# Inner order of three split-precision products in a kernel of graph blocks on one core

## What is computed

```python
def reference(x, adj, nodemask, ...):
    x = _layernorm(x + _L0_gnn_ref(x, adj, W))
    # relu([x, (adj @ x) / deg] @ W.T): x's own part plus the aggregate
    x = _layernorm(x + _L1_gnn_ref(x, adj, W1, b1, W2, b2, W3, b3))
    # three GCN layers: support = x @ W; adj @ support + b; relu after the first two
    x = _layernorm(x + _L2_gnn_ref(x, nodemask, adj, adj, W_qkv, W_out, b_out))
    # 8 heads of 64: softmax plus adjacency and exp(-distance) terms, times values
    x = _layernorm(x + _L3_gnn_ref(x, adj, W_qk, W_v))
    # one gate per node, softmax over the nodes, times values
```

## Time and profile before

| | |
|---|---|
| runs | 1280.2 us median, 1279.27 to 1281.15 |
| the profiled execution | 1280.6 us, span of the core 1278.7 us |
| mean granted TensorE clock | 0.998 of 2.4 GHz |
| TensorE matmuls | 98% of the span, 10732 matmuls and as many weight loads |
| VectorE, ScalarE, GpSimd | 90%, 75%, 14% |

### The profile page before, as it was taken

The page is one execution under the profiler, slowest core; times in us unless marked ns, Lnnn a source line. Parts: engine busy times, 40 slices in busy tenths (PEclk is TensorE's granted clock), DMA queues, the critical chain, the costliest instruction groups (busy, mean ns, idle before and its releaser), DMA issues.

```text
span 1278.7 us, 30231 instructions
## 1 busy us (share of the span) xinstructions
PE 1259.2 (98%) x10732; PEld 1156.0 (90%) x10732; DVE 1155.8 (90%) x3671; ACT 958.4 (75%) x2534; POOL 177.2 (14%) x383
## 2 busy tenths in 40 slices
PE   8999999999999999999999999999999999999997
PEld 7888999999999999999999999999999999999886
DVE  6988999999999999999999999999999999998895
ACT  6677678778778787777787787787787787787773
POOL 0001111101111101111111111011111011111011
PEclk9999999999999999999999999999999999999999
DMA  6110111110111100111100111101111101110000
GB/s 230 35 35 2 35 43 44 44 31 14 44 43 44 43 27 19 43 44 43 44 12 34 43 44 44 43 2 43 44 43 44 43 2 44 43 44 10 10 9 25
DMA packets 42659, 49.06 MB, mean 38 GB/s; under 512 B 16272, under 2 KB 25232, under 8 KB 42512
## 3 DMA queue, kind: packets, MB, share of 16 engines
q1 hardware_dynamic: 42512, 47.14, 11.7%
HBM read 38.68 MB, written 8.39 MB: 37 GB/s over the span
## 4 chain that ended last, share of the span: by engine, by line
PE 94%; DVE 2%; ACT 2%; DMA 1%; issue 1%; POOL 0%; SPq 0%; POOLq 0%; DVEq 0%
PE psum L1551 63%; PE psum L1565 11%; PE psum L1803 9%; PE psum L1761 8%; PE psum L1854 1%; PE psum L1857 1%; ACT work L578 1%; DMA adjT_sb<-in_adjT 0%; DVE bn L929 0%; DMA v_sb<-in_w 0%; DVE x L963 0%; DVE x_pre L1021 0%; POOL rstd L382 0%; DVE x_pre L1187 0%; DVE work L1092 0%
## 5 line engine op out<-in xcount | busy, mean ns | idle before, releaser
L578 ACT ACTIVATE work<-work,shift 128x256 f32<-128x256 f32 x512 | 253.7, 500 | 4.9 <-DVE shift L1092 4.8
L1111 DVE SCALAR_TENSOR_TENSOR work<-work,rsum,extra 128x256 f32<-128x256 f32 x512 | 216.8, 475 | 1.0
L1092 DVE CUSTOM_DVE_ANT_0 work<-psum,minus_big 128x256 f32<-128x256 f32 x512 | 189.0, 417 | 3.0 <-PE psum L1761 2.8
L429 ACT ACTIVATE work<-psum 128x512 f32<-128x512 f32 x256 | 138.0, 598 | 71.6 <-PE psum L1565 71.5
L379 POOL TENSOR_TENSOR mv<-mv,eps 128x2 f32<-128x2 f32 x128 | 31.0, 242 | 1081.7 <-DVE mv L950 1081.7
L1551 PE MATMUL psum<-x2T_h,wqkv_h 128*128 128x256 f32 x512 | 145.6, 284 | 0.0
L429 ACT ACTIVATE sup_h<-psum 128x512 fp32r<-128x512 f32 x124 | 73.2, 590 | 95.2 <-PE psum L1551 95.1
L1551 PE MATMUL psum<-x2T_h,wqkv_l 128*128 128x256 f32 x512 | 143.0, 279 | 0.0
L1551 PE MATMUL psum<-x2T_l,wqkv_h 128*128 128x256 f32 x512 | 142.9, 279 | 0.0
L1565 PE MATMUL psum<-ident,work 128*128 128x128 f32 x1024 | 127.4, 273 | 0.0
L1803 PE MATMUL psum<-work,v_sb 128*64 128x256 f32 x1024 | 124.6, 385 | 0.0
(11 more groups left out here) (189 smaller groups left out, 3798.5 us busy)
## 6 DMA issues: line engine op xcount, KB each, us to landing
xT_sb<-in_xT SPq DMA_DIRECT2D x32, 256.0 KB, 2.6
adjT_sb<-in_adjT SPq DMA_DIRECT2D x32, 256.0 KB, 3.0
adj_sb<-in_adj SPq DMA_DIRECT2D x32, 256.0 KB, 4.0
x_sb<-in_x SPq DMA_DIRECT2D x32, 256.0 KB, 4.3
out<-y_sb SPq DMA_DIRECT2D x32, 256.0 KB, 3.5
work<-in_wqkv SPq DMA_DIRECT2D x1, 1536.0 KB, 9.6
mask_row<-in_nodemask SPq DMA_DIRECT2D x32, 32.0 KB, 4.2
w_raw<-in_w SPq DMA_DIRECT2D x3, 256.0 KB, 5.4
```

The source lines that it names most:

```text
L429: return nc.scalar.activation(dst, src, ACT.Copy, scale=scale)
L578: last = nc.scalar.activation(prob[:, p % 2, i, h], prob[:, p % 2, i, h], ACT.Exp, bias=shift[:, p % 2, h, i:i + 1], scale=-1.0, accum_out ...
L1092: last = V_.tensor_tensor_reduce(out=prob[:, p % 2, i, h], in0=bank(SCORES[p] + h)[:, i * N:(i + 1) * N], in1=minus_big[:, g % 2, i], scal ...
L1111: last = V_.scalar_tensor_tensor(out=prob[:, p % 2, i, h], in0=prob[:, p % 2, i, h], scalar=rsum[:, p % 2, h, i:i + 1], in1=extra[:, g % 2 ...
```

## The change

A new function, `whole_product`, writes a product in one piece: for each t and k the matmuls Lh Rh, Lh Rl, Ll Rh in turn. `self_product` and `support` call it in place of the two parts. `support` loses its argument `part`, and all its waits, the one for the low half among them, stand ahead of its first matmul. All ten places that call `support` are changed alike: the two calls (HI, LO) become one in the same place. The first two of them are shown.

```diff
--- before.py
+++ after.py
@@ -1579,6 +1579,13 @@
                                    late[part], opens=part == HI and t == 0, closes=part == LO and t == NT - 1)
                 return last
 
+            def whole_product(dst, left, right):
+                for t in range(NT):
+                    last = product(dst[:, t * F:(t + 1) * F],
+                                   [(cut(left, A, k, block_of(t)), cut(right, A, k)) for k in range(FT)],
+                                   opens=t == 0, closes=t == NT - 1)
+                return last
+
             def weights(g, number):
                 if g == 0:
                     pe.wait_ge(dve_w, number)
@@ -1610,9 +1617,7 @@
                 weights(g, W0 + 1)
                 pe.wait_ge(dve_xT, once(g))
                 reuse(pe, act_self, once(g - 1))
-                for part in (HI, LO):
-                    last = nodes_product(bank(SELF), fT_of(g), [w[:, :, 0:F] for w in w0], part)
-                last.then_inc(pe_self, 1)
+                whole_product(bank(SELF), fT_of(g), [w[:, :, 0:F] for w in w0]).then_inc(pe_self, 1)
 
             def aggregate(g, part):
                 if not live(g):
@@ -1640,26 +1645,17 @@
                 if part == LO:
                     last.then_inc(pe_sup[0], 1)
 
-            def support(layer, g, part):
-                if not live(g):
-                    return
-                if part == HI:
-                    weights(g, W1 + layer)
-                    if layer == 2:
-                        reuse(pe, dve_qk, nth(g - 1, layer))
-                    if layer == 1:
-                        reuse(pe, dve_gate, once(g - 3))
-                        pe.wait_ge(act_hid_hi[0], once(g))
-                    if layer == 2:
-                        pe.wait_ge(act_hid_hi[1], once(g))
-                else:
-                    if layer == 1:
-                        pe.wait_ge(dve_hid[0], once(g))
-                    if layer == 2:
-                        pe.wait_ge(dve_hid[1], once(g))
-                last = nodes_product(bank(SUP[layer]), hidT_of(g), [w[:, layer] for w in w123], part)
-                if part == LO:
-                    last.then_inc(pe_sup[layer], 1)
+            def support(layer, g):
+                if not live(g):
+                    return
+                weights(g, W1 + layer)
+                if layer == 2:
+                    reuse(pe, dve_qk, nth(g - 1, layer))
+                if layer == 1:
+                    reuse(pe, dve_gate, once(g - 3))
+                pe.wait_ge(act_hid_hi[layer - 1], once(g))
+                pe.wait_ge(dve_hid[layer - 1], once(g))
+                whole_product(bank(SUP[layer]), hidT_of(g), [w[:, layer] for w in w123]).then_inc(pe_sup[layer], 1)
 
             def hidden(layer, g, part):
                 if not live(g):
@@ -1888,8 +1884,7 @@
                 scores(s - 3, 1)
                 attend(s - 4, 2)
                 attend(s - 4, 3)
-                support(1, s - 2, HI)
-                support(1, s - 2, LO)
+                support(1, s - 2)
                 qk(s - 3, 2)
                 support0(s - 1, HI)
                 hidden(1, s - 2, HI)
@@ -1898,8 +1893,7 @@
                 self_product(s - 1)
                 project_out(s - 4, HI)
                 project_out(s - 4, LO)
-                support(2, s - 2, HI)
-                support(2, s - 2, LO)
+                support(2, s - 2)
                 values(s - 3, HI)
                 gcn_out(s - 2, HI)
                 gcn_out(s - 2, LO)
...
```

More of the change, by code:

```diff
@@ L1944, in first_graphs @@
                 keep_busy(7, 11)
-                support(1, 0, HI)
-                support(1, 0, LO)
+                support(1, 0)
                 keep_busy(7, 4)
@@ L1950, in first_graphs @@
                 support0(2, HI)
-                support(2, 0, HI)
-                support(2, 0, LO)
+                support(2, 0)
                 keep_busy(7, 3)
@@ L1964, in first_graphs @@
                 qk(0, 1)
-                support(1, 1, HI)
-                support(1, 1, LO)
+                support(1, 1)
                 scores(0, 0)
@@ L1975, in first_graphs @@
                 values(0, HI)
-                support(2, 1, HI)
-                support(2, 1, LO)
+                support(2, 1)
                 values(0, LO)
@@ L2003, in first_graphs @@
                 attend(0, 3)
-                support(1, 2, HI)
-                support(1, 2, LO)
+                support(1, 2)
                 qk(1, 2)
@@ L2012, in first_graphs @@
                 self_product(3)
-                support(2, 2, HI)
-                support(2, 2, LO)
+                support(2, 2)
                 values(1, HI)
@@ L2051, in last_graphs @@
                 attend(G - 3, 3)
-                support(1, G - 1, HI)
-                support(1, G - 1, LO)
+                support(1, G - 1)
                 values(G - 2, HI)
@@ L2059, in last_graphs @@
                 project_out(G - 3, LO)
-                support(2, G - 1, HI)
-                support(2, G - 1, LO)
+                support(2, G - 1)
                 values(G - 2, LO)
```

## The result

| | before | changed |
|---|---|---|
| median of 20 runs each, us | 1279.41 (1278.88 to 1281.15) | 1282.76 (1280.45 to 1285.32) |
| ratio, 95% interval | 1 | 1.0022 (1.0016 to 1.0028) |
| the profiled execution, us | 1280.6 | 1282.7 |
| its span, us | 1278.7 | 1280.8 |
| mean granted TensorE clock | 0.998 | 0.997 |

A forecast was written before the change was run, and what follows sets the result against it. TensorE's matmuls, 98% of the span, were taken as the bound. Late starts outside the loop, 0.73 + 0.09 + 0.99 + 0.47 + 0.20 = 2.48 us, gave 1282.7 against the median 1280.2; 8 in 10 range 1279.6 to 1285.0.

The forecast's parts named there:

- The wait in the loop: Second and third supports, 28 slots: low halves are ready 1.1 and 1.2 us early, so the wait costs nothing.
- Graph 0, second support, costed at nothing: Starts 0.77 us late, hidden by ScalarE's queue, so 0; were ScalarE free, 0.77.
- Graph 0, third support, 0.73: Starts 0.73 us late with TensorE idle before it and the chain on both sides; paid in full.
- Graph 1, third support, 0.99: Starts 0.99 us late inside an unbroken TensorE stretch, so nothing takes it up.
- the 0.09: Graph 1's second support: starts 45.91 against 45.82, 0.09 us late, added to the sum.
- Graphs 2 and 3, 0.47 and 0.20: Third supports of graphs 2 and 3 start 0.47 and 0.20 us late, both added in full.
- The four terms behind the transposes: Late starts of graph 1's second and third supports and graphs 2 and 3's third supports: 0.09, 0.99, 0.47, 0.20 us.
- a taking up: VectorE's low halves of graphs 1 and 2 come in its own order: only 0.73 remains, 1280.9; chance 0.09.
- Last graph, third support: Starts 0.36 us late, taken up in TensorE's 0.34 us idle at 1211.83: 0, at most 0.36.
- The inner order, 0: Same matmuls in another order within three products: taken as 0, bounds -2.8 and +1.4 us.
- rival on a distance: Loop: own part or second support turns short, 1279.9 or 1281.3, chance 0.16; third support turns long, 1284.1, chance 0.18.
- 1280.2: Median of the runs before, in us, against which the forecast of 1282.7 was set.

The follow-up runs named there:

- graph 0 third: Kernel before with only graph 0's third support as a whole product, its wait ahead: 1280.86 us, ratio 1.0007.
- before with filler: Kernel before with 21 in place of 11 filler transposes ahead of graph 0's second support: 1279.66 us, ratio 0.9998.
- waits only: Kernel before with its old inner order, but supports wait for both halves ahead of the first matmul: 1281.67 us, ratio 1.0013.
- changed with filler: Changed kernel with 21 in place of 11 filler transposes ahead of graph 0's second support: 1281.4 us, ratio 1.0011.
- loop supports: Kernel before with whole products for the supports of graphs 4 to 30 only, x's own part as before: 1279.34 us, ratio 0.9994.
- the sixth: Kernel before with only graph 1's third support as a whole product, its wait ahead: 1280.74 us, ratio 1.0003.
- ends only: Kernel before with whole products, waits ahead, for the supports of graphs 0 to 3 and 31 only: 1282.35 us, ratio 1.0020.
- changed again: The changed kernel itself measured once more, against the kernel before: 1283.57 us, ratio 1.0030.
- own part only: Kernel before with only x's own part written as whole products, no wait moved: 1280.11 us, ratio 0.9999.

## Why the prediction was right, and where its parts were off

**The wait in the loop: right.** Graphs 4 to 30 with whole supports take 0.9994 (0.9985 to 1.0002), and the slot in the profile is as long as before. The cover of 1.1 us ahead of each support was enough.

**Graph 0, second support, costed at nothing: right for what it was costed by, with little to spare.** Where the clock stays up, the stretch from first to second high half is 6.33 and 6.36 with the old wait (graph 0 third, before with filler) and 6.35 and 6.35 with the new. ScalarE's queue hides the 0.77, and only just: in waits only and in changed with filler it takes the result 0.03 and 0.05 us after the product's last matmul ends. In loop supports, where the adjacency load was in time, it took it 0.17 us after that end with the old wait, so there most of the 0.77 would have shown, by estimate. What was missed is that the same 0.77 lengthens TensorE's idle time, and that this can end in a halved clock.

**Graph 0, third support, 0.73: right.** The idle time before it is 1.50, as foretold, and the stretch from second high half to transposes is longer by 0.73 (9.35 to 10.08), by 0.68 where it was the only product changed. Nothing up to the transposes takes it up.

**Graph 1, third support, 0.99: right.** Its start moved from 56.49 to 58.78, 2.29, of which 1.15 was there at the transposes; the second support brought 47.05 - 45.82 - 1.15 = 0.08 of the 0.09, and took 0.04 more itself (1.54 against 1.50; after a wait the second matmul follows the first by 0.19 instead of 0.12). The rest, 1.02, is the third support; the idle time ahead of it is listed as 0.88, since idle is counted from the end of the last matmul and not from when the next could have started. VectorE did not catch up while TensorE stood: graph 1's low half begins 15.77 us after graph 0's transposes before (56.65 - 40.88) and 15.92 after (57.95 - 42.03), and no idle time of VectorE stands ahead of that row.

**Graphs 2 and 3, 0.47 and 0.20: right where they start, and taken back behind.** Between the transposes and graph 2's third support the lateness goes from 1.13 to 1.59; in the four other profiles with all these waits it goes up by 0.46 or 0.47. At graph 3's it goes up by 0.20, in all five. After the wait those products run 1.49 (91.39 - 89.90; 132.18 - 130.69), against 1.36 before (the same product in a slot), so in this kernel each cost 0.13 more than its late start, which was in no term. Then it is given back. The aggregate's part with the low half of `sup` waited for VectorE in the kernel before, and no longer does where the third support ahead of it was late. Before and changed, the two places:

```profile
91.86 0.73 PE L1551 MATMUL psum<-sup_l,adjT_h 128*128 128x256 f32 x4
...
94.50 0.53 PEld L1551 LDWEIGHTS psum<-sup_l,adjT_h 128*128 128x128 f32 x4 [0.21 <-DVE sup_l L900]
94.51 0.72 PE L1551 MATMUL psum<-sup_l,adjT_h 128*128 128x256 f32 x4
```

```profile
94.64 0.63 PE L1551 MATMUL psum<-sup_l,adjT_h 128*128 128x256 f32 x4
...
97.02 0.63 PE L1551 MATMUL psum<-sup_l,adjT_h 128*128 128x256 f32 x4
```

2.78 late at the first, 2.51 at the second. It happens once more behind graph 3's third support, and graph 4's second support is 2.49 late. Less the 1.15 at the transposes, the lateness is 1.13 ahead of graph 2's third support, 1.27 after its aggregate, and 1.34 at graph 4's second support, where the last 0.1 is in kernels with the old waits too. So of these two products nearly nothing stays, while graph 1's term stays whole, in the changed kernel and in the sixth, where it was alone.

The four terms behind the transposes, 0.09 + 0.99 + 0.47 + 0.20 = 1.75 in the forecast, measure 1.34. The four other profiles with all these waits give 1.37 (waits only), 1.31 (changed with filler), 1.34 (ends only) and, from 42.31 to 159.81, 1.36 (changed again). The kernel before has the shortest such stretch of the seven profiles with the old waits (116.14 to 116.40); against their mean the cost is 1.2. The sum is 0.73 + 1.34 = 2.07 instead of 2.48, or 1.9 against the mean. The terms of the forecast that were mis-sized are those of graphs 2 and 3, 0.67 together: it added them in full because no idle stood ahead of those products, and did not look at the wait for VectorE behind them. It had allowed for a taking up, but only at the low halves that the supports themselves read.

**Last graph, third support, taken up: right.** It starts 2.75 late (1211.80 - 1209.05) and the first matmul of the output aggregate 2.40 late:

```profile
1214.23 0.38 PE L1551 MATMUL psum<-sup_h,adjT_h 128*128 128x256 f32 x1
```

against 1211.83 before. Between the two ScalarE copies the support's result: that copy began 2.16 us after the product's start in the kernel before and 1.81 after it in the changed one, so the 0.35 was taken up ahead of it.

**The inner order, 0: right.** In one slot each of the changed kernel, of waits only (old order), of own part only and of loop supports, the second support takes 1.51 to 1.52, the own part 1.41, the third support 1.36. Neither rival on a distance came: in the loop no product that was rewritten changed its distance. The third supports of graphs 2 and 3 did run longer (1.49), but they do so in waits only as well, by 0.08 and 0.13 with the old order inside, so that comes with the wait. One that was not rewritten does: the query-key product behind the second support. Over the 28 slots it ran at the short distance in 12 before, 25 in before with filler, 14 in the changed kernel and in none when the same changed kernel was profiled again (0 of 28 in waits only and own part only too). So the same program gets either; what decides it is not shown (the two profiles may be of different chips). That kernel's last stretch is 1121.3 in one profile and 1122.1 in the other. The last line of the table of stretches, -0.4, is inside this, so no effect of the change is shown by it.

The Trainium skill's rule of "TensorE: Matmul & The Clock Gate" (what happens when a matmul is issued), matmuls stay in program order, is borne out: not one of the matmuls on the high half passed the waiting one.

**The number.** 1282.7 was forecast and 1282.76 measured; that they agree to 0.1 us is luck, though the waits are most of it. The waits give 2.07 in the traces, not 2.48; the halved clock adds 1.25 in the profiled execution, and 1.2 less goes to an earlier first high half (-0.42), the shorter wait for the adjacency load (1.25 - 0.84 = 0.41) and the loop's distances (-0.4): 2.07 + 1.25 - 0.42 - 0.41 - 0.4 = 2.1, the difference of the two spans. The forecast was also set against 1280.2, while 20 runs put the kernel before at 1279.41.

**What stays open.** How much of the slowdown belongs to the clock. The waits are 1.9 to 2.1 us in the traces; the ratio makes it 2.8 and the medians 3.35, so 0.7 to 1.5 is left. With filler the changed kernel is at 1.0011 instead of 1.0022 and 1.0030, which speaks for a share of that size, but waits only, without filler, is at 1.0013 (1.0005 to 1.0022). Every timed execution of the experiments and of the changed kernel has its mean granted clock on record, and this allows an estimate. At 0.998 the mean time is 1282.4 for the changed kernel (8 executions) and 1280.0 for the one before (46); at 0.997 it is 1283.1 (11) and 1281.0 (26). So at the same clock the changed kernel is 2.0 to 2.4 us slower, about the size of the waits. Its mean clock is lower, 0.9973 (26 executions) against 0.9979 (88), and within one kernel 0.001 less goes with 0.9 us more: some 0.5 us. The mean doesn't say where the clock was low, since start and end of every profile are at half clock too (until 11.3 us in the kernel before, until 6.7 in the changed one), and several chips are mixed in it. Whether falls are more frequent in the changed kernel is not shown: three of four unfilled kernels with the late wait had one in their profile, three of six without.

## What to carry to other kernels

Before a wait is drawn to the front of a block of matmuls, compare for every call of it, not for the typical slot, when the operand is ready and when the block begins: here 27 of 28 slots were free, and a few products at the edges paid 2 us, most of it the third supports of graphs 0 and 1. A delay ahead of an engine that is nearly never idle stays, unless a wait for another producer stands close behind it; look at the next low half, not only at this one. And where start-up leaves TensorE idle behind a load, look at the granted clock there in more than one profile: one execution of a kernel doesn't tell what the next will get.

## What was not expected of the hardware

- **Half clock after an idle stretch in start-up.** 1.2 GHz instead of 2.4 in six of 13 profiles, where TensorE stood 2.82 to 3.86 us ahead of graph 0's second support; in the seven others it stood 0.19 to 1.64 us. In ends only the clock fell while it stood, in the five others 0.1 to 1.5 us after it had begun again. Distances of 256-column matmuls went from 0.12 to 0.21 us, in the kernel with the old wait as well. The Trainium skill, "TensorE: Matmul & The Clock Gate", "What's actually happening", has the clock go back to half when the engine has been idle; the trace agrees in the level, 0.50 against 1.00 for the same stretch, and shows that most of the half clock lay over matmuls and not over the idle time. Timeline of own part only:

```profile
25.80 0.45 PE L1551 MATMUL psum<-w_h,hidT_h 128*128 128x256 f32 x1 [2.90 <-ACT hidT_h L429]
26.04 0.42 PE L1551 MATMUL psum<-w_l,hidT_h 128*128 128x256 f32 x1
26.26 0.41 PE L1551 MATMUL psum<-w_h,hidT_h 128*128 128x256 f32 x1
```

- **Within a product the distance keeps, and the same program gets another one in another execution**: 0.113 or 0.118 us for the query-key product, 14 and 0 of 28 slots for the same kernel, 0.8 us over the loop. After a wait the third support ran 1.49 instead of 1.36: the slow first step is 0.08 of it, and the rest is the long distance in place of the short one. In waits only graph 2's ran 1.44, at the short distance, and graph 3's 1.49.
- **Start-up differs between executions by more than the change is worth**: ScalarE's copy of the 1536 KB load begins at 20.41 to 22.80 us in the 13 profiles.
